# Two tiles of the last stage inside the attention's last group, all output weights prepared one stage earlier, and other slots for the special projections

## The reference, cut to what matters

```python
x = x + _layernorm(_L0_attn_ref(_layernorm(x, axis=-1), ...), axis=-1)     # stage A: long convolution
x = x + _layernorm(_L0_ffn_ref(_layernorm(x, axis=-1), ...), axis=-1)      # stage B: gated FFN with LoRA
x = x + _layernorm(_L1_attn_ref(_layernorm(x, axis=-1), Wq, Wkv, Wo, bo))  # stage C, and half of D
x = x + _layernorm(_L1_ffn_ref(_layernorm(x, axis=-1), ...), axis=-1)      # rest of stage D

def _L1_attn_ref(x, Wq, Wkv, Wo, bo):        # 32 heads of 32, 8 groups of keys and values, causal
    scores = jnp.einsum('bhqd,bhkd->bhqk', q, k)
    weights = jax.nn.softmax(scores * (1.0 / HD ** 0.5), axis=-1)
    ctx = jnp.einsum('bhqk,bhkd->bhqd', weights, v)
    return jnp.dot(ctx.transpose(0, 2, 1, 3).reshape(b, t, d), Wo) + bo
```

## Time and profile before

| | us |
|---|---|
| median of 3 runs | 2169.49 |
| lowest and highest | 2166.04, 2169.91 |
| the profiled execution | 2166.32 |
| its span in the profile | 2164.6 |
| TensorE busy | 2007.2 (93%) |
| mean granted clock of TensorE | 0.969 |

### The profile page before, as it was taken

One profiled execution on the slowest core, in us unless ns is written; L12 is line 12 of the kernel. 1 busy time (PEld: TensorE's weight loads), 2 busy tenths in 40 slices (PEclk: granted clock), 3 DMA queues, 4 the chain that ended last, 5 costly groups with the idle time before them and its releaser, 6 DMA issues.

```text
span 2164.6 us, 30708 instructions
## 1 busy us (share of the span) xinstructions
PE 2007.2 (93%) x10444; PEld 1453.2 (67%) x10444; DVE 1410.7 (65%) x3209; ACT 933.2 (43%) x1946; POOL 1069.1 (49%) x918
## 2 busy tenths in 40 slices
PE   5889986999999989999998999899988999999998
PEld 4644545788888879755665566565654687888887
DVE  6877657677777763187774677567776577654433
ACT  5645685233333333125554455455556433323211
POOL 1444586666655630028884488588885243220000
PEclk9999988899999999989999999999998999999999
DMA  6400366233333357522223733333243375553332
GB/s 187 174 7 1 120 230 237 80 129 131 132 129 136 137 199 285 158 64 65 81 79 105 216 94 84 100 90 104 66 138 99 116 241 189 174 171 133 137 125 98
DMA packets 149531, 283.73 MB, mean 131 GB/s; under 512 B 28430, under 2 KB 69262, under 8 KB 149248
## 3 DMA queue, kind: packets, MB, share of 16 engines
q1 hardware_dynamic: 122624, 239.83, 34.8%
q10 hardware_dynamic: 26752, 41.95, 5.8%
HBM read 159.28 MB, written 90.70 MB: 115 GB/s over the span
## 4 chain that ended last, share of the span: by engine, by line
PE 68%; DVE 8%; issue 4%; DMA 3%; ACT 3%; POOL 2%; SPq 2%; ACTq 1%; DVEq 0%; POOLq 0%
PE PS L2100 5%; PE PS L2715 5%; PE PS L2719 5%; PE PS L2716 5%; PE PS L2085 5%; PE PS L2067 5%; PE PS L1135 3%; PE PS L1134 3%; PE PS L1136 3%; PE PS L2043 3%; PE PS L2044 3%; PE PS L2045 3%; PE PS L1184 2%; PE PS L1185 2%; PE PS L1186 2%
## 5 line engine op out<-in xcount | busy, mean ns | idle before, releaser
L2255 ACT ACTIVATE c_P<-PS 128x512 f32<-128x512 f32 (+3 forms) x768 | 349.3, 496 | 343.0 <-PE PS L2085 184.7
L2067 PE MATMUL PS<-c_K,c_Q 96*128 96x512 f32 (+3 forms) x768 | 276.2, 370 | 25.5 <-DVE cst L2392 13.5
L2085 PE MATMUL PS<-c_Q,c_K 97*128 97x512 f32 (+3 forms) x768 | 274.5, 372 | 18.0 <-ACT c_P L2255 10.5
L2498 POOL TENSOR_TENSOR c_S<-c_S,c_P 128x1024 f32<-128x1024 f32 (+3 forms) x94 | 241.6, 2571 | 22.0 <-DVE c_S L2341 12.7
L2085 PEld LDWEIGHTS PS<-c_Q,c_K 97*128 97x128 f32 x768 | 146.7, 193 | 141.8 <-ACT c_P L2255 98.2
L2388 DVE TENSOR_REDUCE cst<-PS 128x1 f32<-128x512 f32 x256 | 175.7, 686 | 82.7 <-PE PS L2067 82.6
L2067 PEld LDWEIGHTS PS<-c_K,c_Q 96*128 96x128 f32 x768 | 149.2, 195 | 81.9 <-DVE cst L2392 32.1
L214 POOL TENSOR_TENSOR maskw<-maskw,mhalf 128x1 f32<-128x1 f32 x64 | 37.3, 582 | 329.7 <-DVE maskw L172 317.4
L2392 DVE CUSTOM_DVE_ANT_0 PS<-PS,maskw,cst 128x128 f32<-128x128 f32 (+3 forms) x256 | 142.9, 558 | 52.5 <-PE PS L2067 33.8
L2475 POOL TENSOR_SCALAR_AFFINE_SELECT c_P<-c_P 128x512 f32<-128x512 f32 x128 | 87.5, 684 | 164.2 <-ACT c_P L2255 164.2
L2392 DVE CUSTOM_DVE_ANT_0 PS<-PS,maskw 128x128 f32<-128x128 f32 (+3 forms) x256 | 124.5, 507 | 65.8 <-PE PS L2067 64.5
(11 more groups left out here) (309 smaller groups left out, 4893.0 us busy)
## 6 DMA issues: line engine op xcount, KB each, us to landing
c_w<-pre_d SPq DMA_DIRECT2D x34, 512.0 KB, 4.4
a_xin<-in_x SPq DMA_DIRECT2D x32, 512.0 KB, 4.3
d_x<-scr SPq DMA_DIRECT2D x32, 512.0 KB, 5.0
c_Q<-c_qh SPq DMA_DIRECT2D x240, 64.0 KB, 2.0
pre_d<-b_pre ACTq DMA_DIRECT2D x28, 512.0 KB, 2.8
scr<-a_xin SPq DMA_DIRECT2D x16, 512.0 KB, 5.8
b_xn<-scr SPq DMA_DIRECT2D x16, 512.0 KB, 5.7
b_x<-scr SPq DMA_DIRECT2D x16, 512.0 KB, 4.8
```

Of the source, the lines that this page charges most:

```text
L2067: e.matmul(bank[:, 0:hi - lo], self.Q4[0:96, 4 * (o % 3) + g, 128 * t:128 * t + 128], self.K4[0:96, HEADS[o % 8], lo:hi], start=True, stop ...
L2085: e.matmul(self.k.bank(i % 3)[:, 0:hi - lo], self.K4[0:97, HEADS[o % 8], 128 * kt:128 * kt + 128], self.Q4[0:97, 4 * (o % 3) + g, lo:hi], ...
L2255: e.activation(self.P[:, R % 3, g, 0:hi - lo], self.k.bank(i % 3)[:, 0:hi - lo], ACT.Exp, scale=SCALE).then_inc(self.exp_s.s, 1)
L2498: e.tensor_tensor(S[:, gs, 512 - n:512], S[:, gs, 512 - n:512], P[:, gs, 0:n], ADD).then_inc(self.psum_s.s, 1)
```

## The change

- Stage B: `PRE` has 36 pieces (all of `wo`), and a piece takes two chunks. The load stands at the end of an odd chunk, the cast right behind the `act_silu` of the next even chunk (ahead of `act_ghi` and `act_xt`), the subtraction ahead of `pool_gf`, the store ahead of the `act_silu` of the next odd chunk, where the next load follows.
- Stage C: all `wo` comes ready from `pre_d` by 16 DMAs of 512 KB at S = 644, 650, ..., 686; `act_wo` and `low_wo` are gone. The slots of `K2`, `7`, `K3` and the second parts of 6 and 11 shift; a new semaphore `half_s` lets the second half of the next weights be loaded once 12 of a job's 16 pieces are done, ahead of the placement of its second part. `sp_mrow` comes ahead of `sp_place` of the same slot. In the `BY_ROUND` groups GpSimd makes both pair sums. The steps of `sp_finish` are 5 slots later in group 9 too.
- Last group: tile 0's 8 pieces stand at S = 711, 715, ..., 739, tile 1's at 745, ..., 761 and between and behind the last products; inputs, casts, subtractions and tile 0's normalisation move there with them.

```diff
+    def pre_at(t, c, step):
+        s = 6 * t + c - 9 - step
+        return s // 2 if s >= 0 and s % 2 == 0 and s // 2 < len(PRE) else None
+    def act_pre_load(self, e, p):
+        if p > 0:
+            e.wait_ge(*self.pre_out(p))
...
+    def act_pre_hi(self, e, p):
+        e.wait_ge(*self.pre_in(p + 1))
+        e.copy(self.pre[:, 0, :], self.raw).then_inc(self.pre_hi.s, 1)
+    def act_pre_store(self, e, p):
+        e.wait_ge(*self.pre_lo(p + 1))
+        e.dma_start(self.k.pre_d[p], self.pre[:, :, :].bitcast(F32)).then_inc(self.pre_out.s, 16)
@@ StageB.act
+                if last is not None:
+                    self.act_pre_store(e, last)
                 self.act_silu(e, t, c)
+                if p is not None:
+                    self.act_pre_hi(e, p)
                 if c in (0, 2):
                     self.act_ghi(e, t - 1, c // 2)
...
-                self.act_pre(e, t, c)
+                if now is not None:
+                    self.act_pre_load(e, now)
@@ tables of slots
-... + [("wo", c) for c in range(4)]
+... + [("wo", c) for c in range(8)]
-JOBS += [... (6, q_slots(172, 2, 188, 2), (194, 204)),
-         ("K2", q_slots(208, 1, 218, 1), (217, 227)), (7, q_slots(231, 1, 241, 1), (242, 260)), ...
-         ("K3", q_slots(405, 1, 415, 1), (414, 424)), (11, q_slots(428, 1, 438, 2), (437, 453)), ...
+JOBS += [... (6, q_slots(172, 2, 190, 2), (194, 206)),
+         ("K2", q_slots(208, 1, 219, 1), (217, 228)), (7, q_slots(231, 1, 243, 1), (242, 260)), ...
+         ("K3", q_slots(405, 1, 416, 1), (414, 425)), (11, q_slots(428, 1, 438, 2), (437, 454)), ...
+WO_IN = {644 + 6 * c: c for c in range(8)}
+TILES = {711 + 4 * n: (0, n) for n in range(8)} | {745 + 4 * n: (1, n) for n in range(5)}
-                self.next_at[slots[15] + 2] = n + 1
+                self.next_at[slots[11] + 1], self.next_at[slots[15] + 1] = (n, 1), (n + 1, 0)
-        late = 5 if S >= 720 else 0
+        late = 5 if S >= 720 or 432 <= S < 480 else 0
@@ StageC.pe_job
+        if q == 11:
+            m.then_inc(self.half_s.s, 1)
@@ StageC.sp
+                if s == 40 and o < 15:
+                    self.sp_mrow(e, o + 1)
                 if S in self.place_at:
                     self.sp_place(e, *self.place_at[S])
...
-                if s == 40 and o < 15:
-                    self.sp_mrow(e, o + 1)
@@ StageC.pool
-                if r == 5:
+                for gs in ([slice(0, 2), slice(2, 4)][:2 if o in BY_ROUND else 1] if r == 5 else ()):
...
-                for q in range(4 if (o, r) in WO_POOL else 0):
-                    self.low_wo(e, WO_POOL[o, r], q)
@@ StageC.dve
-                if s in ((25, 26) if o == 15 else (27, 28)):
+                if s in (27, 28) and o not in BY_ROUND:
...
+                if S == 704:
+                    for half in range(2):
+                        self.then.dve_lo(e, 0, half)
+                if S in (729, 744):
+                    self.then.dve_lo(e, 1, int(S > 729))
+                if S == 746:
+                    self.then.dve_y(e, 0)
@@ StageD
-    def pe_zero(self, e, c):
+    def pe_early(self, e, u, c):
+        k, C, b = self.k, self.before, (6, 3)[u]
+        if (u, c) == (0, 0):
             e.wait_ge(*C.mx_s(768))
+            e.wait_ge(*C.mtc_s(16))
             e.wait_ge(*C.qlo_s(2 * len(JOBS)))
+        if (u, c) == (1, 0):
+            e.wait_ge(*C.evs_s(31))
```

More of the change, by code:

```diff
@@ L1779, in adds, with others, pairs @@
         return first + (r + piece if r == 1 else r + 1 if r < 6 else r - (5 if o in BY_ROUND else 1))
+    @staticmethod
+    def others(o):
+        return o - sum(b < o for b in BY_ROUND)
+    def pairs(self, o, part):
+        return 2 * o - self.others(o) + part + 1
     def dsum_s(self, n, g):
@@ L2623, in sp_second @@
         e.wait_ge(*C.amax_s(768))
-        self.sp_in(e, 2)
         for u in range(1, 3):
@@ L2776, in pe @@
             for half in range(2):
-                if u > 0:
+                if u > 1:
                     self.pe_out(e, u, half)
-                if u == 1 and half == 0:
-                    self.before.pe_sum(e, 31)
                 if half == 0 and NT <= u + 1 < 2 * NT:
@@ L2928, in dve_chunk, with dve_y @@
         e.tensor_tensor(l[:, c % 8, :], self.org[:, :], h[:, c % 8, :].bitcast(F32), SUB).then_inc(self.wlo.s, 1)
-    def first_dve(self, e):
-        C = self.before
-        e.wait_ge(*C.score_s(720))
-        e.wait_ge(*C.amax_s(720))
-        for half in range(2):
-            self.dve_lo(e, 0, half)
+    def dve_y(self, e, u):
+        T, t = self.tail(u)
+        e.wait_ge(*self.out(2 * u + 2))
+        y = self.y(u)
+        if u == 0:
+            e.wait_ge(*self.ldb(1))
+        if u < NT:
+            e.tensor_tensor(y, y, self.bo[:, :], ADD).then_inc(self.biased.s, 1)
+            e.wait_ge(*self.biased(u + 1))
+        T.dve_y(e, self.k.mine["dve"].on(e), t, y)
     def dve_last(self, e, own):
@@ L3000, in pool @@
         k, T0 = self.k, self.T[0]
-        for u in range(1, 2 * NT + 1):
+        for u in range(2, 2 * NT + 1):
             T, t = self.tail(u - 1)
             T.pool_y(e, t)
-            if u == 1:
-                self.before.pool_mul(e, 31)
             if 2 <= u < NT + 2:
```

258 lines of the change are left out of this document (113 added, 145 removed).

## The result

Median of the changed kernel 2156.20 us (2153.32 to 2163.20, 6 runs), of the kernel before beside it 2167.68 us (2164.97 to 2169.91, 6 runs): ratio 0.9949, 95% interval 0.9936 to 0.9961. It is faster by 0.5%, 11.5 us, where 28.5 were forecast (2140). The profiled execution took 2154.80 us, with a span of 2153.0.

What follows compares the result with a forecast made beforehand. TensorE was taken as the bound, with only stage C's stretches leaving gain. Terms +10 - 12 - 8 - 8 - 10.5 = -28.5 us from the profiled 2166.32 give 2137.8, forecast 2140 as median (own range 2130 to 2152; 80% 2122 to 2162).

Steps and rivals of the forecast that it cites:

- Stage B: Stage B (405 to 785): the new order makes TensorE's fold late in 12 tiles; +10 us, at most 37.
- The chain: Stage B, chunk 0's silu to chunk 3's fold: cast, subtraction, store, load, cast and two copies take 9.18 us without handovers.
- seven handovers: Stage B: passing work between engines adds 0.1 us each, 0.7 in all, so the fold starts at 611.8 instead of 611.07.
- rival 1: Stage B hides its new chain, so the sum is -38.5 us, about 2129; 15%.
- Special projections: Groups 3 to 5: weights loaded ahead of placement end two weight waits; -12 us (-6 to -16).
- What may take the gap's place: Groups 3 to 5: SyncE's four placements of 7.5 us and GpSimd's product waiting behind them; pair sum 2.38 us more on GpSimd.
- Group 9: 1335 to 1444: the row of maxima issued ahead of placement and weights ends a 6.38 us gap; -8 us (-5 to -9.5).
- Groups 13 and 14: 1618 to 1657: subtractions leave GpSimd, casts leave ScalarE, pair sum moves to GpSimd; -8 us (-2 to -11).
- Tile 1: Last group: tile 1's 48 matmuls (10.8 us) leave stage D and fit between 1657 and 1707; -10.5 us (-3 to -14).
- rival 2: Attention gaps return as other waits, SyncE or GpSimd the bound in groups 4 and 14; half of 28 us lost, 2154; 20%.
- Rival 4: Last group doesn't take tile 1 and grows by as much as stage D shrinks; 2150; 7%.
- Rival 3: Slower: stage B's chain is late by 1.8 us or more a tile and the clock falls; 2182; 8%.

Runs made afterwards that it cites:

- e4: Changed kernel with ScalarE's weight cast in chunk 2 of stage B behind the tile's copy instead of ahead of it; ratio 0.9940 to the kernel before.
- e1: Changed kernel with group 5's row of maxima issued ahead of K2's 12 placement DMAs instead of behind them; ratio 0.9935 to the kernel before.
- e12: Changed kernel with ScalarE's second four 512 KB reloads one slot later, from 256 instead of 255; ratio 0.9930 to the kernel before.
- e2: Changed kernel with GpSimd's product with the reciprocals in group 5 moved from round 4 to round 7; ratio 0.9953 to the kernel before.
- e9: Changed kernel with group 5's maxima row, stage B's cast, tile 0's subtractions, tile 1's chunks and output-weight loads 3 to 7 reordered; 2139.33 us, ratio 0.9868.
- e7: Changed kernel with the second pair sums of groups 4 and 5 on VectorE again instead of GpSimd; ratio 0.9938 to the kernel before.
- e3: Changed kernel with VectorE's two subtractions for tile 0 in slot 707, behind the last row maxima, instead of 704; ratio 0.9937 to the kernel before.
- e8: Changed kernel with the 8 output-weight loads of 1 MB at slots 665, 670, ... instead of 644, 650, ...; ratio 0.9931 to the kernel before.
- e5: Changed kernel with all 8 chunks of tile 1 behind the last score, instead of 5 between the scores; ratio 0.9971 to the kernel before.
- e6: Changed kernel with tile 1's 5 early chunks at slots 747, 751, ... instead of 745, 749, ...; ratio 0.9941 to the kernel before.

## Why the forecast was right in sign and wrong in size

**Stage B: +10 forecast, +3.9 measured.** The chain and the place were right: e4 takes the loss away. Two steps of the size were not. "To that come seven handovers ... so 0.7 us" is wrong. Tile 9 (ScalarE's timeline, after), which answers to the earlier trace rows:

```profile
604.70 0.55 ACT L1311 ACTIVATE b_g<-PS 128x460 f32<-128x460 f32 x1 [0.33 <-PE PS L1156]
605.33 0.63 ACT L1277 CAST b_pre<-b_raw 128x512 fp32r<-128x512 f32 x1
...
607.35 0.33 ACTq L1281 DMA_DIRECT2D pre_d<-b_pre  x1
...
610.04 0.34 ACTq L1269 DMA_DIRECT2D b_raw<-in_wo  x1
...
612.71 0.62 ACT L1277 CAST b_pre<-b_raw 128x512 fp32r<-128x512 f32 x1 [0.97 <-DMA b_raw<-in_wo]
613.24 0.37 ACT L1318 CAST b_gfh<-PS 115x256 fp32r<-115x256 f32 x1
613.50 0.59 ACT L1254 COPY b_xT<-PS 128x512 f32<-128x512 f32 x1
```

The end of silu to the end of the copy takes 614.09 - 605.25 = 8.84 us, less than the 9.18 without any handover, since ScalarE's instructions overlap by 0.1 and a landing holds its own handover (2.69 and 2.67 us from issue to issue and to the cast). The kernel before had 9.19 us from the end of silu to `pe_fold`, so from tile 9 on, where output weights are treated, no tile is longer than before: there rival 1 holds. And I had let the first cast start right behind silu. In tiles 3 to 8 (query weights, the last with the keys') it waits for its load, as in tile 7 (ScalarE's timeline, after):

```profile
547.65 0.55 ACT L1311 ACTIVATE b_g<-PS 128x460 f32<-128x460 f32 x1 [0.33 <-PE PS L1156]
549.81 0.62 ACT L1277 CAST b_pre<-b_raw 128x512 fp32r<-128x512 f32 x1 [1.60 <-DMA b_raw<-in_wq]
...
558.19 0.59 ACT L1254 COPY b_xT<-PS 128x512 f32<-128x512 f32 x1
```

From silu's end at 548.20 (start and 0.55) to the copy's end at 558.78 it is 10.58 us, 1.39 over 9.19, and TensorE waits 1.15. Twelve times 0.7 was in truth five tiles with 0.2 to 1.5, 4.3 in all. The upper bound was also added up wrongly: with the longest subtraction and landings the terms give 613.64, 2.6 us late without handovers and 3.3 with them, not 3.1.

**Special projections: -12 forecast, -1.0 measured.** The weight waits of the earlier trace rows went, as said. The step that failed is "What may take the gap's place": I named SyncE's four placements and GpSimd's product behind them, and priced them with nothing but the distance to the bound of -6. Two waits came. The row of maxima stands behind K2's placement (5.1 us; e1), which is the very effect that I had priced for group 9 and didn't look for in group 4. And the store of the reciprocals became slow (3.3 to 4.0 us instead of 1.4) because ScalarE's reload now goes out 0.2 us ahead of it instead of 0.9 us behind (e12; why the two changed places was not tried). That store holds up all of SyncE's queue behind it: in e2, with the product out of its way, it was the placement of group 7's queries that came late. With both away e9 has -12.4 for groups 3 to 5. The extra pair sum on GpSimd, which I had also named, is innocent (e7).

**Group 9: -8 forecast, -11.1 in groups 8 and 9**, less 1.8 that groups 6, 7 and 10 to 12 lost: -9.3. The step held, in mechanism and size.

**Groups 13 and 14: -8 forecast, -2.6 measured.** The gap of 3.20 us went, as said. Two costs were mis-sized. The subtractions of tile 0 were priced by the row at "at most 2 x 1.4 = 2.9 us once", 1 us of it in the term; they took 4.74 - 1.38 = 3.4 us more, and TensorE's wait of 3.24 came from them, plus 2.6 us in the stretch behind, where the clock stood at 0.70 (e3). The Trainium skill ("SBUF — State Buffer", "SBUF: two separate sides"), as the prediction cites it, had the mechanism: such a subtraction and a GpSimd instruction that reads SBUF exclude each other for a whole instruction. The traces agree: in the changed kernel's two profiles each subtraction that took longer than 0.7 us ended 0.54 or 0.55 us behind the end of a GpSimd instruction that ran beside it, and moved by three slots the two took 1.79 (e3). What I lacked was the look at how many GpSimd instructions follow each other there: I had priced one, and it was two additions of 2.38 and a select of 0.63. The row of maxima behind 1 MB loads costs 1.4 to 1.6 us (e8), about half of the 3 that I had named for a small DMA. With both orders mended e9 has -5.8 here, at a granted clock of 0.96; the 2.2 us that are left no run shows.

**Tile 1: -10.5 forecast, -1.6 measured.** Tile 1 itself is worth 5.3 us of the 6.75 that stand between the scores (e5). Against it stand the 2.6 us at the lower clock, 2.0 us by chunks in the same slot as the product of values (e6), and an error of mine: "Weight loads tell how full a stretch is, since a full one shows 76.08 of 93, or 82%". Slots 0 to 23 of group 15 now are busy 18.94 of 18.94 us with 11.40 of weight loads, 60%. Products of values have short loads; here are eight of them, matmuls and loads (timelines, after):

```profile
1666.50 1.06 PE L2101 MATMUL PS<-c_P,c_V 128*32 128x512 f32 x8
```

```profile
1666.50 0.16 PEld L2101 LDWEIGHTS PS<-c_P,c_V 128*32 128x32 f32 x8
```

So this stretch is full at 60%, not at 82, and the room was smaller than I took. How many of the missing microseconds that makes was not measured. With both errors of order away e9 has -6.3. What the remaining 4.2 us are, no run separates.

**Sum.** The five orders of e9 bring 2139.33 us where 2140 was forecast, with ratio 0.9868: most of the work that the change takes off TensorE's path is there, and most of what ate it were the orders of SyncE's, ScalarE's, VectorE's and TensorE's lists at five places. That the two numbers meet is partly chance: in e9 stage B loses 0.9 us where the forecast has 10, and the last group gains 6.3 where it has 10.5.

**The rivals.** For the changed kernel itself rival 2 came nearest. Its three terms were to bring 28 us and brought 12.9, so 15.1 were lost, about the half that it named. That its 2154 lies so near the measured 2156.20 is partly luck, since it took stage B at +10 and tile 1 at -10.5, and these two errors (6.1 too much loss, 8.9 too much gain) largely cancel. Rival 4 (the last group gets longer by as much as stage D gets shorter) is close to what was measured there, -1.6, but not for its reason: e5 shows room for most of the five chunks, and e9 gains 6.3. Rival 3 is out.

## What to carry to other kernels

Where an edit takes a wait away, follow every queue in the same stretch to what stands next behind the same kind of blocker. Do so in all stretches in which the edit's pattern occurs: the row behind a placement was known in group 8 and overlooked in group 4. Before an instruction with two SBUF inputs goes into VectorE's list, look up all that GpSimd runs without a break in that slot, and put it behind whatever the critical engine waits for. How full a stretch is can't be told from its share of weight loads, unless it has the same kinds of matmuls as the full stretch it is compared with. Where the profile names no releaser of a wait, look in the kernel for what that instruction waits for, and in the trace for when it landed.
